# Sampling stage of an attention-plus-deformable-convolution kernel: four product buffers, and one row-summing operation for two steps, over 28 kept columns instead of 30

## What is computed

```python
om = conv3x3(x, w_off) + b_off                  # 27 maps: 9 offsets in y, 9 in x, 9 masks
py, px = off_y + row + ky, off_x + column + kx  # one sampling point for each pixel and tap
sampled = bilinear(x, py, px) * sigmoid(mask)   # (B, C, 9, H, W)
out = einsum('bckhw,ock->bohw', sampled, w.reshape(O, C, 9)) + b
return relu(batch_norm(out)) + x
```

## Time and profile before

| | before |
|---|---|
| median of three runs | 865.84 us (865.44 to 867.58) |
| the profiled execution's own time | 861.69 us |
| its span | 859.9 us |
| mean granted TensorE clock | 0.964 |
| sampling stage, first product to last row sum | 322.1 to 833.7 us |
| busy in the span: TensorE, VectorE, ScalarE, GpSimd | 692.2, 719.1, 584.7, 603.3 us |

### The profile page before, as it was taken

How to read it: one execution, slowest core, us unless ns; L and a number is a source line. 1 busy time by engine, 2 the same in 40 slices (tenths; PEclk the granted TensorE clock), 3 DMA queues, 4 the chain that set the end, 5 groups by cost and what they waited for, 6 DMA issues and landing times.

```text
span 859.9 us, 30275 instructions
## 1 busy us (share of the span) xinstructions
PE 692.2 (80%) x12282; PEld 500.2 (58%) x12282; DVE 719.1 (84%) x935; ACT 584.7 (68%) x1089; POOL 603.3 (70%) x401
## 2 busy tenths in 40 slices
PE   5968888885999958888888788888878887777763
PEld 1325565554446647666766666667666666555542
DVE  3469999997322119999999999999999999999975
ACT  2646776774213239788788798888888988777714
POOL 3047888781410008898898998999999999989960
PEclk9989999998999979999999999999999999999976
DMA  4000000000481148555555555565466555555302
GB/s 164 1 0 2 1 0 0 0 0 0 112 204 27 21 106 207 140 156 151 141 140 162 145 158 147 143 166 161 120 167 166 141 157 152 160 146 156 96 4 98
DMA packets 29937, 90.69 MB, mean 105 GB/s; under 512 B 10622, under 2 KB 10750, under 8 KB 29566
## 3 DMA queue, kind: packets, MB, share of 16 engines
q1 hardware_dynamic: 26672, 88.12, 38.3%
q10 hardware_dynamic: 3150, 0.88, 0.5%
HBM read 79.01 MB, written 3.28 MB: 96 GB/s over the span
## 4 chain that ended last, share of the span: by engine, by line
PE 40%; DVE 39%; issue 15%; ACT 2%; DMA 1%; POOL 1%; DVEq 1%; ACTq 0%; SPq 0%; POOLq 0%
PE PS L1128 40%; DVE region L767 19%; DVE region L779 9%; DVE region L645 2%; DVE region L601 2%; DVE region L605 1%; DVE region L620 1%; DVE region L607 1%; PE PS L1210 1%; DVE region L602 1%; DMA region<-px_scratch 1%; ACT region L874 0%; DVE region L575 0%; DVE region L561 0%; DMA cst<-in_consts 0%
## 5 line engine op out<-in xcount | busy, mean ns | idle before, releaser
L1128 PE MATMUL PS<-region 64*64 64x144 f32 (+3 forms) x10112 | 456.4, 292 | 112.6 <-issue 81.2
L1128 PEld LDWEIGHTS PS<-region 64*64 64x64 f32 (+1 forms) x10112 | 342.2, 134 | 219.9 <-issue 198.3
L767 DVE TENSOR_TENSOR region<-PS,region 128x864 f32<-128x864 f32 x384 | 381.2, 1046 | 12.4 <-PE PS L1128 12.3
L509 POOL TENSOR_TENSOR region<-region 128x768 f32<-128x768 f32 x128 | 202.4, 1581 | 67.5 <-DVE region L767 67.5
L513 POOL TENSOR_TENSOR region<-region 128x864 f32<-128x864 f32 x128 | 224.0, 1750 | 18.7 <-POOL region L509 0.4
L1006 ACT ACTIVATE region<-region 128x1152 f32<-128x1152 f32 x128 | 149.2, 1165 | 34.3 <-PE PS L1128 30.6
L1003 ACT ACTIVATE region<-region,cst 128x1152 f32<-128x1152 f32 x128 | 159.2, 1244 | 7.7 <-DMA region<-px_scratch 6.3
L779 DVE TENSOR_REDUCE region<-region 128x32 f32<-128x960 f32 x128 | 145.9, 1140 | 1.5 <-POOL region L513 1.5
L1037 ACT ACTIVATE region<-x,cst (+2 forms) x288 | 86.7, 414 | 0.0
L1128 PE MATMUL PS<-wg,xp 64*64 64x144 f32 x1024 | 82.6, 286 | 5.0 <-issue 4.9
L432 POOL TENSOR_TENSOR region<-region,cst 128x1024 f32<-128x1024 f32 x32 | 61.4, 1917 | 31.4 <-PE PS L1203 25.3
(11 more groups left out here) (118 smaller groups left out, 590.6 us busy)
## 6 DMA issues: line engine op xcount, KB each, us to landing
region<-px_scratch SPq DMA_DIRECT2D x256, 288.0 KB, 4.3
out<-region SPq DMA_DIRECT2D x4, 512.0 KB, 3.0
region<-xp SPq DMA_DIRECT2D x8, 140.2 KB, 2.9
region<-xp SPq DMA_DIRECT2D x8, 140.1 KB, 2.8
region<-xp SPq DMA_DIRECT2D x8, 140.0 KB, 2.9
cst<-in_consts SPq DMA_DIRECT2D x1, 1104.0 KB, 8.6
region<-xp SPq DMA_DIRECT2D x8, 132.0 KB, 2.7
region<-xp SPq DMA_DIRECT2D x8, 131.9 KB, 2.7
```

Source lines behind the costliest of these rows:

```text
L509: pool.tensor_tensor(two_rows[:, :, :, 0:2 * THIRD - KEEP], two_rows[:, :, :, 0:2 * THIRD - KEEP], two_rows[:, :, :, KEEP:2 * THIRD], ALU. ...
L767: v.tensor_tensor(uu[:, 2 * u:2 * u + 2, :, THIRD * t:THIRD * (t + 1)], PS[:, 2 * t:2 * t + 2, 0:THIRD * C].rearrange("p h (a o) -> p h o ...
L1128: return nc.tensor.matmul(o, l, r, start=start, stop=stop)
```

## The change

It raises the number of product buffers from three to four, and puts the fourth over `two` and `bd`, which move to the end of `region2`. It lowers the kept columns from 30 to 28, so that the first addition on GpSimd adds columns 28 to 53 onto 0 to 25 (26 columns instead of 24, at a distance of 28 instead of 30); the second addition is unchanged, at a distance of 54. And the row sum takes two steps at once: behind `products(n)` of every odd n from 3 on, VectorE sums steps n-3 and n-2 with one operation over 64 rows of 28 columns. The last pair of steps is summed behind the loop.

```diff
-KEEP = THIRD + 3
+KEEP = THIRD + 1
...
-UB = 3
+UB = 4
...
-        bd = sb("bd", [P, 6, P])
...
-        two = sb("two", [P, 2, 2 * CH])
-        rs = two[:, 0, CH:CH + P * 2].rearrange("p (h a) -> p h a", h=2)
...
-        cut2 = cutter("region2", 2 * 2 * KK * W + UB * 2 * NA * C)
+        cut2 = cutter("region2", 2 * 2 * KK * W + (UB - 1) * 2 * NA * C + 4 * CH + 6 * P)
+        cut2(2 * 2 * KK * W + (UB - 1) * 2 * NA * C)
+        two = cut2(4 * CH).rearrange("p (u k) -> p u k", u=2)
+        bd = cut2(6 * P).rearrange("p (s k) -> p s k", s=6)
+        rs = two[:, 0, CH:CH + P * 2].rearrange("p (h a) -> p h a", h=2)
+        cut2(None)
...
-            def totals(line, g):
-                return os4[:, bass.ds(line, 2), bass.ds(g, 1), :].rearrange("p y g o -> p y (g o)")
+            def totals(line, g, rows=2):
+                return os4[:, bass.ds(line, rows), bass.ds(g, 1), :].rearrange("p y g o -> p y (g o)")
...
                 def add(n):
                     b = 2 * (n % UB)
-                    dve.wait_ge(fold_ready, done(n))
-                    v.tensor_reduce(totals(2 * (n % STEPS), n // STEPS), uu[:, b:b + 2, :, 0:KEEP], AX.X, ALU.add).then_inc(os_ready, 1)
+                    dve.wait_ge(fold_ready, done(n + 1))
+                    v.tensor_reduce(totals(2 * (n % STEPS), n // STEPS, 4), uu[:, b:b + 4, :, 0:KEEP], AX.X, ALU.add).then_inc(os_ready, 2)
...
                     products(n, 2 * (n % STEPS), n % UB)
-                    if n > 0:
-                        add(n - 1)
-                add(PAIRS * STEPS - 1)
+                    if n >= 3 and n % 2 == 1:
+                        add(n - 3)
+                add(PAIRS * STEPS - 2)
```

## The result

The changed kernel takes **887.21 us** (median of 4 runs, 885.84 to 888.67), against 865.64 us for the kernel before in the same comparison (864.70 to 867.58). The ratio is 1.0247, with a 95% interval of 1.0218 to 1.0275: 21.6 us slower. I had said 859.1, and a range of 853.5 to 865.0. The profiled execution took 885.87 us, with a span of 884.0; its mean granted clock is 0.934. One execution of the kernel before, in the slow state at 3466.99 us, counts in no ratio.

What follows compares the result with a forecast made beforehand. The prediction took VectorE to bound the sampling stage, with GpSimd close behind. Its terms, -12.8 + 3.5 + 1.0 + 1.6 = -6.7 us, took the median from 865.84 to 859.1 us, range 853.5 to 865.0.

Steps and rivals of the forecast that it cites:

- What bounds the kernel now: Sampling stage: VectorE bounds it at 15.81 us per chunk of four steps; GpSimd close behind, needing about 15.0 us.
- The first addition on GpSimd: Sampling stage, GpSimd: 64 more columns cost +0.11 us per step, chunk 15.45 us, level with VectorE; counted as nothing.
- the stage gets longer: Sampling stage: GpSimd becomes the bound, its chunk exceeding 15.81 us, if L509's first addition exceeds 1.78 us; chance 0.06.
- The row sum: Sampling stage, VectorE: one sum for two steps takes 1.92 us instead of 2.12, 64 times; -12.8 us.
- The part on the fourth buffer: Sampling stage: the later sum removes a 1.5 us wait for GpSimd's fold and lets GpSimd lag; by itself brings nothing.
- What the uneven rhythm costs: Sampling stage: back-to-back products leave TensorE's refill 0.75 us slack, so its gaps reach VectorE more; +3.5 us, bounds 0 and +9.
- Start and end: Sampling stage's edges: four steps of products before the first sum, +1.0 us; later last fold and longer last sum, +1.6 us.
- no change: Whole kernel: gaps cost +7 instead of +3.5 and the 64-row sum runs at 1.98 us; 864 to 866 us; chance 0.13.

## Why the prediction was wrong

- **What bounds the kernel now** was right: VectorE, with GpSimd 0.8 us a chunk behind. That second number carried the result, as it is the room that the first addition had.
- **The first addition on GpSimd is the step that failed.** It was taken from a line through 24 and 27 columns as +0.11 us, or 15.45 us a chunk of GpSimd, with the second addition as the upper bound, "as many columns as the new one can cost at most". It measured +0.43 us, which made the chunk 16.69 us and GpSimd the bound. The line was drawn through two points at distances 30 and 54, both of the cheap kind, and the change moved the distance to 28, which I noted in the description of the change and did not price. A bound by nearest rows holds only for what those rows have in common with the new operation. At distance 26 it costs 1.72 us, 0.03 above the line: all but 0.03 us of the miss is the distance. The Trainium skill's estimate in the prediction, 0.14 us more, is what distance 26 measured (1725 - 1581 ns), and at distance 28 it misses as well, since it too has no term for the distance.
- The rival in which **the stage gets longer** had the right place (L509, each step) and the right threshold (1.78 us); the measured 2.01 is well over it, and (2.01 - 1.78) x 128 = 29 us is near the 28 us that the chunks lost. It had 0.06, because I looked for its cause in the width of a row.
- **The row sum**, -12.8 us. Its duration was right: 2.01 us, or 1.93 from start to start where nothing waits. What I missed is that the change turns the products' wait for a buffer into a wait for the instruction just in front. That is 0.15 us for a pair, 9 us, nearly three quarters of the term. In the changed kernel GpSimd hides this; with the distance mended it is what takes the gain away. The part on the fourth buffer looked only at the wait that is lifted, that for the fold, and not at what the products' own wait names with four buffers.
- **What the uneven rhythm costs**, +3.5 us: with the distance mended VectorE waits for TensorE 7.8 us between 340 and 850 us, in 19 pieces, against 2.7 in 5: +5.1 us, within the bounds.
- **Start and end.** At the end, from the last product's end to the last sum's end pass 5.49 us at distance 26 (827.21 + 5.88 = 833.09 to 836.56 + 2.02 = 838.58 in that trace) instead of 3.75: +1.7, where +1.6 was said. At the start the first sum begins 12.63 us after the first product; 12 products back to back would take 11.5, so TensorE held it up by 1.1 us, and before by 0.6 (6.37 us for 6 products): +0.5 instead of +1.0.
- With the distance mended and the wait priced the sum would be -12.8 + 9 + 3.5 + 2.6 = +2.3 us; that kernel measured +0.23% or 2.0 us, with an interval from -0.8 to 4.8.
- The rival **no change** has a slip in its sum: -6.7 + 3.5 + 3.8 is +0.6 us, not 0 to -2. It decides nothing here.

## What to carry to other kernels

The price of a two-input operation on GpSimd can hang on how far its operands lie apart, so slices that are re-cut for another engine's sake should be timed at the new distance. For additions like these (float32, the output over the first input, rows 81 columns apart) a distance that leaves 1 or 2 modulo four columns is the cheap one; other types, row lengths and separate outputs were not tried. When buffers are added or work is grouped, look at which instruction a wait now names: if it is the one directly in front on the same engine, the overlap of the two is gone. Here one independent instruction between them brought it back. And when an engine has 5% of room, price everything that lands on it before the gain on the other engine is counted.

## What the runs showed that I had not expected

- **Distance.** GpSimd's addition of float32 columns, in rows 81 columns apart, costs 0.28 to 0.33 us more for 768 to 864 elements (16 to 20%) at distances of 24, 27, 28, 47, 48, 51 and 52 columns than at 25, 26, 29, 30, 49, 50, 53 and 54. It does not change with the start column in these rows, or with what VectorE runs beside it (24 at 28 took 1862 to 1898 ns in all its 16 places; 26 at 28 took 2009 ns beside the long sums and 2008 beside the short ones). The Trainium skill (SBUF — State Buffer, Specifications) speaks of 16-byte lines, four float32, at whose crossing an access pays. The period of four agrees with that, but the page does not say why a distance of one column less is dear too and one more is not, and no run here shows the mechanism.
- **A wait for the instruction in front** costs VectorE 0.11 to 0.18 us here (1.17 to 1.24 us from sum to product against 1.06): 0.08 us of overlap, and 0.03 to 0.10 until the next instruction begins.
- **The clock.** The profile of the changed kernel has a granted clock of 0.934, that of the kernel before 0.964; in mid-stage it is 0.95 and 1.00. TensorE was busy 78% there instead of 82 to 84: its 12282 matrix products in the whole kernel are as many as before, and the stage is 26 us longer. Its products read 308 ns in the mean instead of 292. GpSimd's chunk has no idle in it, so this decides nothing in mid-stage; what it costs by itself was not tried.
